# Values out of PSUM: one VectorE instruction in place of a ScalarE copy and a GpSimd addition

## The reference

```python
qh = (q_in @ wq + bq).reshape(b, q_len, H, K)
kh = (kv_in @ wk + bk).reshape(b, t, H, K)
vh = (kv_in @ wv + bv).reshape(b, t, H, K)
kh = concatenate([kh, broadcast(bias_k)], axis=1)      # one more key and value,
vh = concatenate([vh, broadcast(bias_v)], axis=1)      # the same for all tokens
logits = einsum('bqhk,bthk->bhqt', qh, kh) / scale
weights = softmax(logits, axis=-1)
ctx = einsum('bhqt,bthk->bqhk', weights, vh).reshape(b, q_len, H * K)
return ctx @ wo + bo
x = x + cross_attention(layer_norm(x), xf, ...)        # twice
```

## Time and profile before

| | |
|---|---|
| time, median of 3 runs | 1415.94 us (1415.51 to 1418.8) |
| profiled execution | 1415.35 us, span 1413.2 us |
| mean granted clock of TensorE | 0.976 |
| PE busy | 1334.0 us (94%), 14427 matmuls |
| PEld busy | 1189.8 us (84%) |
| DVE busy | 904.8 us (64%), 1792 instructions |
| ACT busy | 611.8 us (43%), 1045 instructions |
| POOL busy | 587.3 us (42%), 521 instructions |
| first and second layer | about 35 to 500 and 501 to 965 us of the span |

### The profile page before, as it was taken

One profiled execution on the slowest core, in us unless ns is written; L12 is line 12 of the kernel. 1 busy time (PEld: TensorE's weight loads), 2 busy tenths in 40 slices (PEclk: granted clock), 3 DMA queues, 4 the chain that ended last, 5 costly groups with the idle time before them and its releaser, 6 DMA issues. The chain is left out here.

```text
span 1413.2 us, 33171 instructions
## 1 busy us (share of the span) xinstructions
PE 1334.0 (94%) x14427; PEld 1189.8 (84%) x14427; DVE 904.8 (64%) x1792; ACT 611.8 (43%) x1045; POOL 587.3 (42%) x521
## 2 busy tenths in 40 slices
PE   3999999999999799999999999987998999997898
PEld 3898888888888688888888888977887989996787
DVE  6567767676767866767666767685323588886322
ACT  3534343434444554343434444364223256665421
POOL 4524334144144543414414324364651055554654
PEclk8999999999999999999999999997999999998999
DMA  7011011011010101101101011000000000002000
GB/s 241 4 36 39 1 39 39 1 38 39 1 39 2 38 1 39 39 2 38 38 2 39 2 38 38 2 1 27 1 1 8 1 2 2 2 2 64 4 31 30
DMA packets 31764, 35.91 MB, mean 25 GB/s; under 512 B 955, under 2 KB 29187, under 8 KB 31619
## 3 DMA queue, kind: packets, MB, share of 16 engines
q1 hardware_dynamic: 31394, 33.70, 7.6%
q10 hardware_dynamic: 226, 0.10, 0.0%
HBM read 31.70 MB, written 2.10 MB: 24 GB/s over the span
## 5 line engine op out<-in xcount | busy, mean ns | idle before, releaser
L332 POOL TENSOR_TENSOR V<-V,DV 128x512 f32<-128x512 f32 x128 | 164.0, 1281 | 534.5 <-ACT V L500 534.5
L168 PE MATMUL bank<-SRC_HI,WHI 128*128 128x512 f32 x576 | 230.2, 400 | 4.3 <-PEq L262 4.3
L169 PE MATMUL bank<-SRC_LO,WHI 128*128 128x512 f32 x576 | 229.4, 398 | 0.0
L170 PE MATMUL bank<-SRC_HI,WLO 128*128 128x512 f32 x576 | 228.8, 397 | 0.0
L578 DVE STREAM_TRANSPOSE PRT<-PR 32x256 f32<-32x256 f32 x512 | 223.2, 436 | 8.3
L596 DVE TENSOR_TENSOR CLO<-bank,CHI 128x512 fp32r<-128x512 f32 x128 | 82.4, 686 | 135.9 <-ACT CHI L513 135.9
L492 ACT ACTIVATE QT<-bank,PB 128x512 f32<-128x512 f32 x128 | 87.8, 688 | 177.8 <-PE bank L170 177.8
L168 PE MATMUL bank<-WHI,CHI 128*128 128x256 f32 x512 | 152.0, 297 | 4.4 <-DVE CLO L596 4.0
L168 PE MATMUL bank<-WHI,SRC_HI 128*128 128x256 f32 x512 | 150.4, 294 | 0.0
L170 PE MATMUL bank<-WHI,CLO 128*128 128x256 f32 x512 | 145.1, 283 | 0.7 <-issue 0.7
L169 PE MATMUL bank<-WLO,CHI 128*128 128x256 f32 x512 | 144.9, 283 | 0.0
(11 more groups left out here) (170 smaller groups left out, 3009.7 us busy)
## 6 DMA issues: line engine op xcount, KB each, us to landing
W<-in_wall SPq DMA_DIRECT2D x18, 1024.0 KB, 5.6
VROW<-in_vrow SPq DMA_DIRECT2D x18, 256.0 KB, 6.1
V<-in_ctx SPq DMA_DIRECT2D x4, 512.0 KB, 5.8
X<-in_x SPq DMA_DIRECT2D x4, 512.0 KB, 6.8
mlp_w<-in_w SPq DMA_DIRECT2D x2, 1024.0 KB, 7.7
out<-X SPq DMA_DIRECT2D x4, 512.0 KB, 2.9
BO<-in_borow SPq DMA_DIRECT2D x1, 256.0 KB, 7.0
W<-in_qw SPq DMA_DIRECT2D x1, 256.0 KB, 4.3
```

What stands on the lines that cost most here:

```text
L168: e.matmul(dst, a_hi, b_hi, start=start, stop=False, **kw)
L169: e.matmul(dst, a_hi, b_lo, start=False, stop=False, **kw)
L170: return e.matmul(dst, a_lo, b_hi, start=False, stop=stop, **kw)
L332: e.tensor_tensor(vs, vs, DV[a][:, :].unsqueeze(1).to_broadcast([P, 2, 2 * K]), ALU.add).then_inc(v_shift, 1)
```

## The change

The ScalarE copy of the values out of PSUM and the GpSimd addition of the row DV become one VectorE addition that reads PSUM and DV and writes V. The first of the two (tiles 0 and 1) stands behind the transposes and ahead of the norm and the rounding of weights, the second behind the rest of the context and ahead of the maximum. The semaphore v_shift goes; PV waits for v_out, as the next slot's query projection already does for its banks. On GpSimd the split of weights no longer has the two additions ahead of it.

```diff
@@ gpsimd, slot
                         if front:
-                            for j in range(2):
-
-                                e.wait_ge(v_out, 2 * n + j + 1)
-                                vs = V[at % 2][:, 2 * j:2 * j + 2, :]
-                                e.tensor_tensor(vs, vs, DV[a][:, :].unsqueeze(1).to_broadcast([P, 2, 2 * K]),
-                                                ALU.add).then_inc(v_shift, 1)
                             if g == 1:
                                 split(pair + 1, 1 - a)
@@ tensor, slot
-                            e.wait_ge(v_shift, 2 * n)
+                            e.wait_ge(v_out, 2 * n)
                             e.wait_ge(pt_out, n)
@@ scalar, slot
-                        def values_out(j):
-                            e.wait_ge(v_done, 2 * n + j + 1)
-                            e.activation(V[at % 2][:, 2 * j:2 * j + 2, :],
-                                         PROJ[j][:, :].rearrange("p (t n) -> p t n", n=256),
-                                         ACT.Copy).then_inc(v_out, 1)
-
                         if at == 0:
                             norm_sqrt(e, norm, *norm_now)
-                        if front:
-                            values_out(0)
...
-                        if front:
-                            values_out(1)
@@ vector, slot
+                        def values_out(j):
+                            e.wait_ge(v_done, 2 * n + j + 1)
+                            e.tensor_tensor(V[at % 2][:, 2 * j:2 * j + 2, :],
+                                            PROJ[j][:, :].rearrange("p (t n) -> p t n", n=256),
+                                            DV[a][:, :].unsqueeze(1).to_broadcast([P, 2, 2 * K]),
+                                            ALU.add).then_inc(v_out, 1)
+
...
                             i.then_inc(pt_out, 1)
+                        if front:
+                            values_out(0)
                         if bridge and gb == 0:
...
                                                 ALU.subtract).then_inc(c_lo, 1)
+                        if front:
+                            values_out(1)
                         if norm_now is not None and not front:
```

More of the change, by code:

```diff
@@ L227, in program @@
             bo_in = sem("bo_in")
-            v_shift, bo_added = sem("v_shift"), sem("bo_added")
+            bo_added = sem("bo_added")
             vec_turned, vec_copied = sem("vec_turned"), sem("vec_copied")
```

## The result

| | before | after |
|---|---|---|
| time, median | 1415.94 us (1415.51 to 1418.8) | 1423.53 us (1422.59 to 1426.06) |
| ratio after to before, 95% interval | | 1.0053 (1.0038 to 1.0068) |
| profiled execution, span | 1415.35, 1413.2 us | 1424.29, 1422.3 us |
| mean granted clock | 0.976 | 0.973 |

What follows compares the result with a forecast made beforehand. TensorE's matmuls bound ordinary slots; VectorE delays TensorE at layer turns. Terms -2.8 + 1.0 - 0.1 + 3.1 + 6.8 + 1.6 = +9.6 us on the 1413.2 span: 1422.8, or 1425.5 on the median; range 1418.5 to 1432.

Steps and rivals of the forecast that it cites:

- What goes: 128 ScalarE copies and 128 GpSimd additions (164 us) are off the path, but GpSimd's work holds VectorE's product, costing 0.20 us.
- What comes: 128 VectorE additions reading PSUM and SBUF, 0.69 us each, 88 us in all on VectorE.
- Ordinary slots: Slots outside the layer turn: additions cost nothing, and the product freed behind weight splits returns 0.20 us in 14 slots, -2.8 us.
- Slot 4: Each layer's last round: the earlier GpSimd output-bias addition holds VectorE's product, PV waits 0.5 us; +1.0 us, bounds 0 and 1.5.
- Slot 6: Last rounds: first layer's norm unheld, -1.4 us; second layer's product held and transposes later, +1.3; together -0.1, from -1.5 to +0.5.
- Slot 7: Last rounds: norm waits behind the first addition, product held 0.7 us more, transposes 1.57 us later; two layers +3.1, at least +1.8.
- Slot 0: Start of each layer: the first addition waits for values(0) ahead of the norm, delaying TensorE's turning 3.42 us; two layers +6.8.
- The clock: Behind the new 3.4 us idle time at each layer's start, the clock probably falls: +1.6 us, bounds 0 and 3.8.
- (a): Rival: faster, 1411.8 us, because the start of each layer costs nothing and only the freed lock remains; 6%.
- (b): Rival: the order holds, but small holds in the layer turn fall luckily and the clock stays up; +5, near 1420; 16%.
- (c): Rival: VectorE becomes the bound in ordinary slots; 0.3 us over in 56 slots would give 1442 us; 6%.
- (d): Rival: the clock falls longer, or a further hold in the slots before a PV; 1431 us and more; 8%.

Runs made afterwards that it cites:

- experiment 3: Kernel before the change, with GpSimd's split of weights moved ahead of its two value additions in slots 1 and 5: 1413.63 us, ratio 0.9982.
- experiment 4: Kernel after the change, with GpSimd's output-bias addition of slot 4 also waiting for that slot's transposes: 1420.93 us, one run.
- experiment 6: Kernel after the change, with five unused VectorE additions more ahead of the second new one in 48 ordinary slots: 1457.91 us, one run.
- Experiment 1: Kernel after the change, with the first new addition moved behind the norm in slot 0 of each layer: 1414.35 us, ratio 0.9990.
- experiment 9: Kernel before the change, with VectorE only waiting for values(0) ahead of the norm in slot 0, no work added: 1429.14 us, ratio 1.0099.
- experiment 5: Kernel after the change, with one unused VectorE addition more ahead of the second new one in 48 ordinary slots: 1423.47 us, ratio 1.0040.
- experiment 8: Kernel after the change run again without edit, on another chip where the kernel before took 1418.55 us: 1423.36 us, ratio 1.0039.
- experiment 2: Kernel after the change, with the first new addition moved behind the norm in slots 0, 6 and 7: 1415.32 us, ratio 0.9991.
- experiment 7: Kernel after the change, new additions placed later in slots 0, 6, 7, GpSimd's slot 4 bias and slots 6, 7 row products delayed: 1410.52 us, ratio 0.9948.
- experiment 10: The change with additions and GpSimd work placed later in the turn, plus slot 5's bias addition waiting for the next product: 1408.55 us, ratio 0.9954.

## Why the prediction was right, point by point

**What goes.** Held. ScalarE's copies were worth nothing, GpSimd's only through the hold on VectorE. The freed product gave 1.6 us in the seven slots of the first layer, and in experiment 3 2.4 of the 2.8 us forecast, without VectorE's additions. The lock, argued from one row in the prediction, is shown by experiments 3 and 4: moving the GpSimd instruction in time, and nothing else, takes the product from 1.84 to 0.72 and from 2.15 to 0.69 us.

**What comes.** 0.69 us taken, 677 to 692 ns measured. The Trainium skill (VectorE: DVE Perf Modes, The TRN2 errata) has 120 + 512 cycles for a PSUM source, an estimate of 0.66 us; the trace doesn't agree, with a median of 687 ns.

**Ordinary slots.** No cost, as reckoned; 13.84 to 13.91 us in all of them. The idle time before the maximum went from 0.79 to 0.19 us. The small hold of the product by the row products, 0.3 us, didn't come (345.97 above, 0.69 us).

**Slot 4.** +1.0 forecast, 0.57 and 0.56 measured. Waits before PV of 0.49 us in both layers, 0.5 forecast. Right mechanism, by experiment 4.

**Slot 6.** In the first layer -1.4 forecast, -1.6 measured, with 0.80 us of wait left out of 2.20. In the second +1.3 forecast, +1.0 measured:

```profile
930.49 1.16 PE L398 MATMUL bank<-PRT,V 64*64 64x64 f32 x64 [0.68 <-issue]
...
934.98 1.09 PE L137 MATMUL bank<-ident,XN 128*128 128x128 f32 x8 [0.62 <-DVE XN L128]
```

Both parts of the step can be seen, the transposes late (0.68) and V0's share (0.62).

**Slot 7, the mis-sized term.** +3.1 for two layers forecast, +2.3 measured, 1.16 and 1.18. The row products L163 and the product, GpSimd and VectorE in after:

```profile
489.10 2.94 POOL L163 TENSOR_TENSOR SRC_LO<-HT,SRC_HI 128x512 fp32r<-128x512 f32 x2 [10.55 <-ACT SRC_HI L152]
...
489.75 1.17 DVE L563 TENSOR_TENSOR PR<-ex,ri 128x512 f32<-128x512 f32 x1
```

The general shift there is 1.91 us (L137 of slot 6, above). Beside it the product came 0.69 us later, 0.9 forecast, and L163 1.28 later, 1.6 forecast, and it held the product for 0.48, 0.7 forecast. 0.69 and 0.48 are the 1.17 that slot 8's PV was late. Queued instructions of VectorE start closer together than their durations add up to (0.60 us for 0.68, in the lines of experiment 6), and the reckoning had V1, the maximum and `sub` end to end. That this is the whole 0.3 is argued, not tested. The wait of slot 8 became 6.49 where about 6.8 was forecast.

**Slot 0.** 3.42 us a layer forecast, 3.40 and 3.40 measured, by the step's own chain: values(0) at 44.00, V0 to 44.69, the norm to 48.5, the turning at 48.65. Experiment 1 undoes it by moving V0, experiment 9 makes it by the wait alone.

**The clock.** +1.6 forecast, +1.1 and +0.5 measured. Of the two lengths that the prediction weighed, both occurred: 6.8 us at 1.2 GHz in the first layer, 3.4 in the second. In each trace that has an idle time of 3.2 us or more in slot 0 (after, and experiments 4, 5, 6, 8 and 9) the clock fell behind it in both layers, and in the traces of before and of experiments 1, 2, 3, 7 and 10, which have no such wait there, it did not. The other premise, that the clock stays up after the 2.20 us of slot 6, holds for the trace of before alone: after 2.22 and 2.23 us in the same place, in experiments 3 and 9, it fell. So whether 2.2 us of waiting cost the clock differed between executions, while 3.2 us or more did so in all 12 cases of the six traces.

**The sum.** +9.6 forecast; the ledger has +7.0 up to the end of the second layer. Of the 2.6 between them slot 7 makes 0.8, slot 6 0.5, the place of the low clock between the layers 0.4, and the splits 1.1 (-3.9 in the ledger for -2.8; 0.66 of that is an idle time at 596.77 that the trace of before has and, with 0.39, that of experiment 9, and whose cause isn't known). Slot 4 and the clock are within 0.1 each, slot 0 within 0.04. The span's forecast, 1422.8 against 1422.3, is closer than the terms are, and that is luck: 2.1 us were lost in stages that the change doesn't touch (2.8 at the copy, less 0.7 elsewhere). On the medians the forecast is 2.0 too high (+9.6 for +7.6 measured, +7.0 in the ledger), and beside the +4.8 of experiment 8 it is 4.8 too high.

**The rivals.** (a) fell, by the wait itself. (b) did not hold: the holds of slots 4 and 6 came as reckoned and the clock fell. (c) fell in experiment 5, and experiment 6 shows where it would begin. (d) did not occur in after, but its mechanism, a longer hold and a longer wait in slot 0, is what experiment 9 shows at 1429.14.

**What stays open.** Why the low clock lasts 3.4 us in one run and 6.8 in another for the same wait, and why 2.2 us of waiting brings it in one execution and not in another. Why the copy at the start of the resampler took 1.12 us in one execution and 2.86 in the others, with the same GpSimd work beside it. And what of the best version's gain beyond slot 0 each of its edits brings, since they were not run one by one. The -0.4 between slot 8 and the next slot 0 is put down to the clock without a test.

## What to carry to other kernels

An instruction given to an in-order engine brings its wait along. Before moving an evacuation to another engine, look in each kind of slot, the rare ones too, at what stands behind the wait and who needs it: here some 60 of 64 slots took the additions for nothing, and the two slots 0, with the low clock behind them, cost more than the net result. Where an engine runs ahead of its consumers, put the newcomer behind the work that ran ahead; and read the engines that are relieved for what they held up, since starting them earlier can move a hold onto another slot.

## What the runs showed of the hardware

That a VectorE step with a single tensor input is held by GpSimd too was used in the prediction for slot 6 and forgotten in the expectation of experiment 9: L128 took 3.32 us for four steps beside two GpSimd additions (46.58 to 49.11), and 1.38 with none beside it. The prediction had quoted the Trainium skill (SBUF — State Buffer, Who interferes with whom) only for one with a single input, by which it doesn't contend. The same section excepts the modes that use both ports and counts `tensor_scalar`, which L128 is, among the operations that can enter them and so contend. The trace agrees with that, by 3.32 against 1.38.

The other way round, GpSimd was the one held in after: the two row products beside an unheld product of VectorE,

```profile
345.23 2.23 POOL L318 TENSOR_SCALAR tmp<-W,PH 128x256 f32<-128x256 f32 x2
```

took 2.23 us where they took 1.82 in the same slot before, and the product kept its 0.69. And VectorE's queued instructions overlap by some 0.08 us each: additions of 0.68 us start 0.60 apart, so that five more a slot bring 3.0 us and not 3.4, of which idle time and slack took in all but 0.7.
